# A projection stage that takes x in once, chunk by chunk, and prepares the second batch under the first one's value tiles

## What is computed

```python
xn = _gn(x)                                   # G=32 groups: (x - mean) / sqrt(var + 1e-5)
q, k, v = (einsum('bnd,hed->bhne', xn, W) for W in (Wq, Wk, Wv))     # 8 heads LB, 8 heads LA, E = 64
s = where(mask, q @ k.T / sqrt(64), min)      # LB: i >= j, LA: i <= j
o = softmax(s) @ v
out = x + concat(o_lb, o_la) @ Wo.T
```

## Time and profile before

| | us |
|---|---|
| median of three runs | 3290.93 (3289.3 to 3291.39) |
| profiled execution | 3290.62 |
| its span | 3288.8 |
| TensorE busy | 3104.2 |
| VectorE busy | 1996.7 |
| ScalarE busy | 1591.7 |
| POOL busy | 1271.9 |

### The profile page before, as it was taken

One profiled execution on the slowest core, in us unless ns is written; L12 is line 12 of the kernel. 1 busy time (PEld: TensorE's weight loads), 2 busy tenths in 40 slices (PEclk: granted clock), 3 DMA queues, 4 the chain that ended last, 5 costly groups with the idle time before them and its releaser, 6 DMA issues.

```text
span 3288.8 us, 49072 instructions
## 1 busy us (share of the span) xinstructions
PE 3104.2 (94%) x14472; PEld 2510.5 (76%) x14472; DVE 1996.7 (61%) x3540; ACT 1591.7 (48%) x3173; POOL 1271.9 (39%) x996
## 2 busy tenths in 40 slices
PE   4999799799999969999999999999999999999998
PEld 3788688678888846777777777787777777777786
DVE  6222211421121168788878787887888788788875
ACT  2210111211121136666666666666666666666665
POOL 2000000200000045556556565655655565556554
PEclk9999899899999979999999999999999999999999
DMA  7546534553453464343334333433432343334330
GB/s 241 149 123 148 162 123 103 166 154 115 99 148 105 97 134 97 68 99 85 71 71 105 75 70 80 101 76 68 102 82 71 76 103 74 67 87 98 72 69 22
DMA packets 354509, 333.55 MB, mean 101 GB/s; under 512 B 276480, under 2 KB 276480, under 8 KB 342016
## 3 DMA queue, kind: packets, MB, share of 16 engines
q1 hardware_dynamic: 354304, 331.41, 40.5%
HBM read 213.91 MB, written 117.44 MB: 101 GB/s over the span
## 4 chain that ended last, share of the span: by engine, by line
PE 55%; DVE 7%; issue 2%; DMA 0%; ACT 0%; DVEq 0%; SPq 0%; ACTq 0%
PE rows L1033 11%; PE max L968 7%; PE scores L1001 7%; PE acc L1019 7%; PE acc L1015 7%; PE acc L1017 7%; PE scores L996 7%; DVE o_full L937 3%; DVE part_max L889 1%; PE scores L999 1%; PE side L978 1%; DVE inv L916 1%; DVE inv L923 1%; DVE max L883 0%; DVE wo_l L907 0%
## 5 line engine op out<-in xcount | busy, mean ns | idle before, releaser
L686 POOL TENSOR_TENSOR p_low<-probs,p_high 128x512 fp32r<-128x512 f32 (+2 forms) x960 | 1215.5, 1278 | 874.0 <-ACT p_high L822 801.5
L818 ACT ACTIVATE probs<-scores 128x512 f32<-128x512 f32 (+3 forms) x1280 | 683.9, 534 | 614.1 <-PE scores L1001 601.7
L889 DVE TENSOR_REDUCE part_max<-max 128x1 f32<-128x512 f32 (+3 forms) x1280 | 765.3, 602 | 196.6 <-PE max L968 176.6
L822 ACT ACTIVATE p_high<-scores 128x512 fp32r<-128x512 f32 (+3 forms) x1280 | 680.3, 531 | 0.0
L968 PE MATMUL max<-k,q 128*128 128x512 f32 (+3 forms) x1280 | 481.9, 377 | 79.4 <-DVE part_max L889 61.6
L326 DVE TENSOR_TENSOR stage_l<-proj,stage_h 128x512 fp32r<-128x512 f32 x192 | 132.3, 690 | 685.1 <-ACT stage_h L318 660.5
L318 ACT ACTIVATE stage_h<-proj 128x512 fp32r<-128x512 f32 x192 | 114.6, 598 | 805.8 <-PE proj L264 425.1
L1001 PE MATMUL scores<-q,k 128*128 128x512 f32 (+3 forms) x1280 | 488.4, 382 | 0.0
L996 PE MATMUL scores<-q,k 128*128 128x512 f32 (+3 forms) x1280 | 470.2, 367 | 0.3 <-ACT p_high L822 0.3
L1019 PE MATMUL acc<-p_low,v 128*128 128x512 f32 (+3 forms) x1280 | 468.3, 366 | 0.0
L1015 PE MATMUL acc<-p_high,v 128*128 128x512 f32 (+3 forms) x1280 | 465.9, 364 | 0.6 <-DVE p_low L686 0.6
(11 more groups left out here) (86 smaller groups left out, 4293.7 us busy)
## 6 DMA issues: line engine op xcount, KB each, us to landing
xs<-xT SPq DMA_DIRECT2D x64, 512.0 KB, 4.9
qk_h<-stage_h SPq DMA_DIRECT2D x128, 256.0 KB, 2.6
qk_l<-stage_l SPq DMA_DIRECT2D x128, 256.0 KB, 3.0
q<-qk_h SPq DMA_DIRECT2D x64, 512.0 KB, 4.9
k<-qk_h SPq DMA_DIRECT2D x64, 512.0 KB, 6.8
w_raw<-wqk SPq DMA_DIRECT2D x32, 512.0 KB, 4.0
v_h<-stage_h SPq DMA_DIRECT2D x64, 256.0 KB, 2.6
v_l<-stage_l SPq DMA_DIRECT2D x64, 256.0 KB, 3.1
```

The costliest lines, as they stand in the source:

```text
L686: eng.tensor_tensor(p_low[:, n % 4, part], probs[:, n % 4, part], p_high[:, n % 4, part].bitcast(F32), ALU.subtract).then_inc(done, 1)
L818: nc.scalar.activation(probs[:, n % 4, 0:cols], scores[n % 2][:, 0:cols], ACT.Exp, scale=SCALE).then_inc(exp_done, 1)
L822: nc.scalar.activation(p_high[:, n % 4, 0:cols], scores[n % 2][:, 0:cols], ACT.Exp, scale=SCALE).then_inc(high_act, 1)
L889: nc.vector.tensor_reduce(part_max[:, s % 2, at, m:m + 1], max_bank[n % 2][:, 0:cols], AX.X, ALU.max).then_inc(max_read, 1)
```

## The change

Statistics, normalization and split of batch 0 go chunk by chunk as x comes in, and x of batch 0 is loaded once, into 12 places: the 4 of `xs` and 8 in `x_first`, which lies where `vh` and `vl` will be. The first half chunk of a chunk is normalized by VectorE, the second by ScalarE (`Identity` with scale and bias); both low parts are made by POOL. TensorE multiplies seven tiles chunk by chunk (the eighth bank holds the sums of the statistics) and tile 7 behind them; mean and variance of chunk c+2 are summed between its tiles of chunk c. Value weights are loaded into the slots of `xs` and have their own semaphores. The statistics of batch 1 are closed between value tiles of batch 0, LA, and its chunks are normalized and split there: the first 8 units hold tokens 0 to 1023 of all chunks, the next 8 the other tokens, the last of them under the first tiles of batch 1, which are multiplied tile by tile in the order `FIRST_ORDER`. The core of the diff (the closures `columns`, `staged`, `place`, `loads` give the slot and the count of a half chunk; the bodies of `gather`, `centred`, `variance`, `inverted` and `normal_x` are the instructions of before on a range of chunks):

```diff
+X_PLACES = 12
+FIRST_ORDER = (0, 1, 4, 5, 2, 3, 6, 7)
+        def unit(b, h):
+            return (h // 2, h % 2) if b == 0 else (h % NC, h // NC)
+        def wait_x_low(eng, b, h):
+            if b == 0:
+                eng.wait_ge(x_low_pool, h + 1)
+            elif h % 2 == 0:
+                eng.wait_ge(x_low_pool, X_UNITS + h // 2 + 1)
+            else:
+                eng.wait_ge(x_low_dve, h // 2 + 1)
 # SyncE
             def load_x(b, again, h):
+                if b == 0 and h >= X_PLACES:
+                    wait_x_low(sp, 0, h - X_PLACES)
+                elif b == 1 and h < X_SLOTS:
+                    sp.wait_ge(v_low, again * V_RAWS + h + 1)
+                elif b == 1 and again:
+                    wait_x_low(sp, 1, h - X_SLOTS)
+                elif b == 1:
+                    sp.wait_ge(x_counted, X_UNITS + h - X_SLOTS + 1)
+            def load_v(b, kind):
+                for k in range(V_RAWS):
+                    if (b, kind) == (0, LA):
+                        sp.wait_ge(x_counted, 2 * X_UNITS - X_SLOTS + k + 1)
+                    elif kind == LA:
+                        sp.wait_ge(v_low, 2 * V_RAWS + k + 1)
+                    else:
+                        wait_x_low(sp, b, X_UNITS - X_SLOTS + k)
+                    sp.dma_start(xs[:, k, :], wv[kind, k]).then_inc(v_loaded[k], 16)
             for h in range(X_UNITS):
                 load_x(0, False, h)
-                if h in FIRST_BEHIND:
+                if h in (1, 3):
+                    load_w(wqk[h // 2], h // 2)
+                    if kind == LB:
+                        load_later(b, kind, 0)
+                        if b == 1:
+                            for h in range(X_UNITS - X_SLOTS, X_UNITS):
+                                load_x(1, True, h)
+                        for at, t in enumerate(FIRST_ORDER):
+                            store_qk(b, kind, t // 4, t % 4, tile(b, kind, at))
+                            if at == 3:
+                                load_v(b, kind)
+                            if at == 6:
+                                load_later(b, kind, 1)
+                    else:
+                        one(0, 0, True)
+                        load_v(b, kind)
+                        one(1, 1, True)
+                        if b == 0:
+                            for h in range(X_SLOTS):
+                                load_x(1, True, h)
 # POOL
-            for b in range(B):
-                for h in range(0, X_UNITS, 2):
-                    low_x(pool, b, h, x_low_pool)
+            for h in range(X_UNITS):
+                low_x(pool, 0, h, x_low_pool)
+            for h in range(0, X_UNITS, 2):
+                low_x(pool, 1, h, x_low_pool)
 # TensorE
+            def first_blocks_of_all():
+                for c in range(2):
+                    sum_mean(c, slice(c, c + 1))
+                    sum_var(c, slice(c, c + 1))
+                pe.wait_ge(w_low, 2)
+                for c in range(NC):
+                    for half, tiles in enumerate((FIRST_ORDER[:4], FIRST_ORDER[4:7])):
+                        wait_x_low(pe, 0, 2 * c + half)
+                        for k, t in enumerate(tiles):
+                            last = product(t, c, products)
+                            if c == NC - 1:
+                                last.then_inc(tile_done, 1)
+                            if half == 0 and k == 3 and c + 2 < NC:
+                                sum_mean(c + 2, slice(c + 2, c + 3))
+                            if half == 1 and k == 1 and c + 2 < NC:
+                                sum_var(c + 2, slice(c + 2, c + 3))
+                pe.wait_ge(var_ready, NC)
+                for c in range(NC):
+                    last = product(7, c, products)
+                last.then_inc(tile_done, 1)
+            def first_blocks_again():
+                for at, t in enumerate(FIRST_ORDER):
+                    pe.wait_ge(out_low, tile(1, LB, 0) - 8 + t + 1)
+                    for c in range(NC):
+                        if at % 4 == 0:
+                            wait_x_low(pe, 1, at // 4 * NC + c)
+                        last = product(t, c, products)
+                    last.then_inc(tile_done, 1)
 # value tiles of TensorE
+                        if (b, kind) == (0, LA):
+                            if t == 1:
+                                pe.wait_ge(out_low, tile(b, kind, V_TILES))
+                                sum_mean(NC, slice(0, NC))
+                            if t == 3:
+                                sum_var(NC, slice(0, NC))
+                            if t == 7:
+                                pe.wait_ge(var_ready, NC + 1)
 # ScalarE and VectorE, batch 1 under the value tiles of batch 0, LA
+        AGAIN = {8: (0, 1), 9: (2, 3), 11: (4, 5), 12: (6, 7)}
+            def high_x(b, h):
...
+                    act.wait_ge(x_normal, NC + h + 1)
+                    act.wait_ge(tile_done, tile(0, LA, V_TILES + (half + 1) * TOK // 2))
 # ScalarE, batch 0
+            for c in range(NC):
+                root(c, slice(c, c + 1))
+                act.wait_ge(offset_ready, c + 1)
+                n = place(0, 2 * c + 1)
+                nc.scalar.activation(staged(n), staged(n), ACT.Identity, bias=offset[:, c:c + 1],
+                                     scale=inverse[:, c:c + 1]).then_inc(x_normal_act, 1)
+                high_x(0, 2 * c)
+                high_x(0, 2 * c + 1)
 # VectorE, batch 0
+            gather(0, slice(0, 1), 2)
+            for u in range(2):
+                split_block(dve, False, u, u, 0)
+            for c in range(NC):
+                chunk = slice(c, c + 1)
+                centred(c, chunk)
+                if c + 1 < NC:
+                    count_x(0, 2 * c + 2)
+                variance(c, chunk)
+                if c + 1 < NC:
+                    count_x(0, 2 * c + 3)
+                inverted(c, chunk)
+                nc.vector.tensor_scalar(offset[:, chunk], group_mean[:, chunk], inverse[:, chunk], -1.0,
+                                        ALU.mult, ALU.mult).then_inc(offset_ready, 1)
+                normal_x(0, 2 * c)
+                if c + 1 < NC:
+                    gather(c + 1, slice(c + 1, c + 2), 2 * c + 4)
```

More of the change, by code:

```diff
@@ L219, in _, with product, sum_mean @@
             products = ((wh, xh), (wh, xl), (wl, xh))
+            def product(t, c, of):
+                u, q = t // 4, t % 4
+                for w, x in of:
+                    last = nc.tensor.matmul(bank[t][:, :], w[:, u, c, :], x[:, c, q * NQ:(q + 1) * NQ],
+                                            start=(c == 0 and w is wh and x is xh), stop=(c == NC - 1 and w is wl))
+                return last
+            def sum_mean(k, chunks):
+                pe.wait_ge(channel_ready, k + 1)
+                reached(pe, var_ready, k)
+                nc.tensor.matmul(bank[7][:, chunks], average[:, :], channel[:, chunks, 0],
+                                 start=True, stop=True).then_inc(mean_summed, 1)
@@ new lines, in sum_var @@
+            def sum_var(k, chunks):
+                pe.wait_ge(spread_ready, k + 1)
+                nc.tensor.matmul(bank[7][:, NC + chunks.start:NC + chunks.stop], average[:, :], spread[:, chunks],
+                                 start=True, stop=True).then_inc(var_summed, 1)
+            def first_blocks_of_all():
[18 more added lines that the diff above has]
+                last.then_inc(tile_done, 1)
@@ L339, in one @@
                     if more:
-                        split_block(eng, high, u, n + raw(b, kind, V_RAWS), n * 4 + tile(b, kind, 4))
+                        split_block(eng, high, u, n + raw(b, kind, 0), n * 4 + tile(b, kind, 4))
+                if kind == LB:
+                    for at, t in enumerate(FIRST_ORDER):
+                        between(kind, "first", at)
+                        part_out(eng, t, tile(b, kind, at))
+                        if at == 5:
+                            split_block(eng, high, 0, raw(b, kind, 0), tile(b, kind, 6))
+                    split_block(eng, high, 1, raw(b, kind, 1), tile(b, kind, 8))
+                else:
+                    one(0, 0, True)
+                    one(1, 1, True)
@@ L343, in weights_and_tiles @@
+                split_v(eng, high, b, kind)
                 blocks(eng, b == B - 1 and kind == KINDS - 1, one)
                 for t in range(TOK):
[L345 to L346 removed]
+                    between(kind, "before", t)
                     part_out(eng, t, tile(b, kind, V_TILES + t))
[L349 to L356 removed]
+                    between(kind, "behind", t)
@@ L374, in _, with count_x @@
+            weights_and_tiles(act, True, 0, between_first)
+            weights_and_tiles(act, True, 1, between_second)
         @block.vector
         def _(dve):
+            def count_x(b, h):
+                c, half = unit(b, h)
+                n = place(b, h)
+                dve.wait_ge(x_loaded[n], 16 * loads(b, False, h))
+                for q in range(2):
```

(9 more changed lines are left out.)

279 lines of the change are left out of this document (139 added, 140 removed).

## The result

| | before | after |
|---|---|---|
| median, us | 3291.16 (3289.3 to 3292.9) | 3252.05 (3242.84 to 3260.79) |
| ratio, 95% interval | | 0.9881 (0.9843 to 0.9919) |
| profiled execution, its span | 3290.62, 3288.8 | 3242.84, 3241.0 |
| first matmul of the pair / end of the pair | 44.7 / 98.1 | 23.9 / 83.7 |
| restart behind the pair | 101.84 | 88.25 |

It is faster: 47.8 us in the profiled execution, 39.1 between the medians. The four times after are two near 3243 and two near 3260, a spread of 18 us where before had 3.6; that spread is one of the things to explain. The forecast was 3242, with a range from 3220 to 3259; the median lies in that range, and above the 3234 to 3250 that the sum itself spans.

What follows compares the result with a forecast made beforehand. TensorE, busy 94% of the span, was taken as the bound, with time to gain only at stops or low clock. Part A 48.0 plus Part B 0.5 gave 48.5 us off 3290.6: 3242, range 3220 to 3259.

Steps and rivals of the forecast that it cites:

- Part A: From the second pair of blocks to the projection's end: stops at block 10 and the change of batch go, 48.0 us gained.
- what is late next: After block 10's stop, SyncE waits for value-weight splits with block 12's load queued behind; costed at nothing.
- (3): Change of batch: second batch not ready, TensorE stops as before, 28.4 us come back, 3270; chance 0.05.
- (4): Weights of block 10 or 12 late because SyncE stands in a new wait, 21.8 us come back, 3264; chance 0.04.
- (5): First pair: ring closes over one chunk instead of two, 17.0 us a chunk, slower, up to 3302; chance 0.03.
- Part B: First pair of blocks: chunks pass four engines in a ring, 9.2 us each; restart at 101.3 against 101.84, 0.5 us gained.
- the two-hold value of 10.3: First pair: chunk period in us if two VectorE smalls are held behind different POOL low parts.
- rival (1): First pair: smalls not held and clock stays up, 6.7 us a chunk, 17.5 us less, 3225; chance 0.16.
- rival (2): First pair: TensorE's clock stays at half throughout, 11.4 us a chunk, 3258 to 3263; chance 0.08.
- period of the normalizations 8 to 10.3 us: Sign of being right, in the first pair: time between successive normalizations, one per chunk.
- no stop of TensorE over 3 us from there to the end of the projection: Sign of being right: no TensorE stop over 3 us from the first pair's end, near 100, to the projection's end.
- last projection matmul near 1105: Sign of being right: the projection's last matmul comes near 1105 us, against 1154.37 before.

Runs made afterwards that it cites:

- the long execution: The changed kernel, unaltered, executed and profiled again against its own first profile: 3260.37 us.

## Why the prediction came out

**Part A: right.** Restart to last matmul went from 1052.5 to 1007.8, 44.8 us, forecast 48.0. Of the 3.2 us between, the slow restart is 0.8 (6.8 us at 0.55 of the clock lose 3.1, where 2.3 was set aside). The rest is the value tiles, four stretches of 88.1, 88.5, 88.1 and 88.1 us instead of 87.2, 4.0 us in all, where 1.5 was set aside for the two statistics products. About 0.5 of the 4.0 is theirs, in the second stretch; 3.5 is the wider distance of the value products, a term that the forecast put at nothing by taking every tile at 5.44. The reading that the losses were queue and change of batch, and the step "what is late next", held: no wait for weights at block 10 or 12, and none at the change of batch. Rivals (3) and (4) are out, and so is (5). A miss within it: the stop at block 10 was priced at 21.8 us as if it were the value weights' alone; by themselves they give 16.3 there, and the wait of 3.3 us with its slow restart, 5.2 together, needs the rest of the change to go.

**Part B: the period of a chunk was mis-sized.** The first half chunk was normalized at 19.8 and the first matmul came at 23.9, forecast 21.4 and near 25. The period was forecast as 9.2, "the middle of 8.0 and 10.3". No chunk sits at the middle: with the clock up a chunk takes 7.0 us on the mean of two, since one instruction is held in each and it is in turn the normalization and a small; with the clock down it takes 9.98, since two smalls are held. The rows of a held instruction were read rightly, and the two-hold value of 10.3 was near. What the working lacked is that the two unknowns, hold and clock, are not independent: in the long execution each brings on the other. What the prediction gives from the Trainium skill (SBUF — State Buffer, section Who interferes with whom), that an instruction with one SBUF input is not held, agrees with the counts (0.67 to 0.70 us each, beside POOL too) and not with the normalization; the section leaves certain modes out, as said above. In the first profile the pair ended at 83.7 instead of 99.5, near rival (1), though a small is held in every second chunk; of these 15.8 us the period makes 7 x (9.2 - 7.0) = 15.4. The restart came at 88.25 instead of 101.3. In the long execution the two are 100.4 and 104.77, not far from the forecast. That one's 3260 is the time of rival (2), but only part of its mechanism: the clock falls in every chunk, for 3.4 us of it and not throughout, so a chunk takes 9.98 and not 11.4, and attention adds 12.9 (2129.6 in that profile). The wait for weights behind the pair was 4.4 us, 1.8 in the sum.

**What was not in the sum: attention, 10.5 us.** No row of before showed it as a risk, but the view of waits had the neighbour: 25.2 us in 10 waits for nothing but issue, one at each loop turn. The forecast took code that isn't touched to cost what it did. It was luck, and not the sum, that brought the profiled execution to 3242.84 beside a forecast of 3242.1: 13.6 us instead of 0.5 at the restart, 44.8 instead of 48.0 behind it, 10.5 lost in attention, 13.6 + 44.8 - 10.5 = 47.9 (47.8 in the times). The median, 3252, lies higher by what the loop of holds and clock costs in other executions.

**What would have shown it.** A "period of the normalizations 8 to 10.3 us" came true only where the loop ran (in the first profile they come 4.9 and 9.1 us apart in turn); "no stop of TensorE over 3 us from there to the end of the projection" failed at the weights behind the pair (4.4); the "last projection matmul near 1105" was 1096.0 in the first profile, and 1105.1, 1105.0, 1111.3 and 1098.5 in the others.

## What to carry to other kernels

Where a short instruction of VectorE stands in a ring with POOL and TensorE, give it one SBUF tensor (`tensor_scalar` with a scalar of each partition): here that took 10 us off the median, and the spread went from 6.6 us (18 in the changed kernel) to 3.5. It is shown for one column, not for 1024. Look at the spread of the times beside the median: a spread that grows with a change can come from a stage that runs in two ways, and a price at the middle then fits neither of them. Where a change alters the number of instructions ahead of a loop, compare the waits for issue at the loop's turns before believing that untouched code costs the same.

## What was unexpected of the hardware

The place of a loop head in VectorE's instructions was worth 10.5 to 11.4 us of attention in 3290, in one of the tests with 29 writes of one column as the only edit. An address that differs by 64 bytes changed the distance of the matmuls that read the tile, 0.229 to 0.234 us on the mean, 6.4 us over the four stretches of value tiles and 6.7 from restart to last matmul (1013.5 against 1006.8). And the same program, level to 0.2 us up to one restart, kept TensorE's clock in one execution and lost it in another; in the slow chunks TensorE worked 7.1 of 10 us, more than it waited, started at full clock and lost it 0.7 to 1.8 us later. The row of the granted clock can miss a stretch, too: it says 1.00 for the pair of after, where ten matmuls in a row come 0.43 us apart (24.46 to 28.73), the distance that they have where the row says 0.50 or little more (54.27 to 56.83 in the long execution).
